# Reordering an attention layer: an earlier transpose, smaller products between row maxima, and a new prologue

## The reference, cut to what matters

```python
# layer 0, for each of B = 16 batches; x is [B, N = 1024, C = 256], adj is [N, N]; hd = C / 4 = 64
fea = transpose(x)                       # [C, N]
c_adj = mean(fea, over C)                # one number a node
A_s = a symmetric function of |c_adj[n] - c_adj[m]|     # written with sigmoid, the kernel uses tanh
g = relu((fea @ (adj * A_s)) * para)     # [C, N]
q = the four heads of transpose(g);  k, v = heads of x @ kv_w
attn = softmax(q @ k^T * scale);  out = attn @ v
x = layernorm(x + out)
# layer 1: A_hat = adj with its diagonal raised by one, normalised by degrees; agg = A_hat @ x
h = relu(batchnorm(agg @ W1^T + b1)); x = layernorm(x + batchnorm(h @ W2^T + b2))
```

## Time and profile before

| | |
|---|---|
| median of 3 runs | 3024.26 us (3023.43 to 3026.23) |
| the profiled execution | 3025.48 us, its span 3023.7 us |
| PE busy | 2794.8 us, 92% |
| PEld, DVE, ACT, POOL busy | 62%, 68%, 55%, 37% |
| mean granted TensorE clock | 0.97 of full |
| batch 3, from its first graph product to that of batch 4 | 130.03 us |

### The profile page before, as it was taken

The page is one execution under the profiler, slowest core; times in us unless marked ns, Lnnn a source line. Parts: engine busy times, 40 slices in busy tenths (PEclk is TensorE's granted clock), DMA queues, the critical chain, the costliest instruction groups (busy, mean ns, idle before and its releaser), DMA issues. The chain is left out here.

```text
span 3023.7 us, 38970 instructions
## 1 busy us (share of the span) xinstructions
PE 2794.8 (92%) x12308; PEld 1878.4 (62%) x12308; DVE 2047.3 (68%) x2981; ACT 1667.0 (55%) x2148; POOL 1127.6 (37%) x492
## 2 busy tenths in 40 slices
PE   6999999999999999999999999999499999989964
PEld 4565665656566565655656566565388888868853
DVE  5777777777777777777778777775534233338877
ACT  5666565665656666565666656564422222237768
POOL 1736446373644637355373644627200000000012
PEclk9999999999999999999999999999799999999975
DMA  4131212213122231312223121220322322305548
GB/s 132 57 105 60 83 63 73 89 57 115 56 80 69 64 111 48 102 63 73 72 74 104 59 83 63 73 76 23 112 84 98 111 83 97 111 18 185 186 161 284
DMA packets 154317, 276.19 MB, mean 91 GB/s; under 512 B 12192, under 2 KB 95136, under 8 KB 152224
## 3 DMA queue, kind: packets, MB, share of 16 engines
q1 hardware_dynamic: 154272, 275.62, 28.9%
HBM read 178.79 MB, written 62.98 MB: 80 GB/s over the span
## 5 line engine op out<-in xcount | busy, mean ns | idle before, releaser
L281 POOL TENSOR_TENSOR psum<-psum,probs 128x1024 f32<-128x1024 f32 x320 | 855.5, 2674 | 171.0 <-ACT probs L342 144.1
L342 ACT ACTIVATE probs<-sc_ps 128x1024 f32<-128x1024 f32 x512 | 507.5, 1024 | 458.6 <-PE sc_ps L779 449.7
L507 DVE TENSOR_REDUCE mx<-mx_ps 128x1 f32<-128x512 f32 x768 | 494.3, 685 | 215.3 <-PE mx_ps L747 206.1
L795 PE MATMUL pv_ps<-probs,v 128*64 128x512 f32 x2048 | 490.7, 602 | 0.0
L779 PE MATMUL sc_ps<-qa,ka 128*128 128x512 f32 x1024 | 385.7, 408 | 0.0
L779 PE MATMUL sc_ps<-qb,kb 128*128 128x512 f32 x1024 | 373.3, 395 | 6.5 <-DMA qb<-row 6.5
L281 POOL TENSOR_TENSOR psum<-probs 128x1024 f32<-128x1024 f32 x64 | 183.2, 2863 | 511.6 <-ACT probs L342 511.6
L747 PE MATMUL mx_ps<-ka,qa 128*128 128x512 f32 x768 | 288.9, 435 | 15.4 <-DVE mx L507 10.7
L795 PEld LDWEIGHTS pv_ps<-probs,v 128*64 128x64 f32 x2048 | 130.2, 137 | 232.7 <-issue 195.6
L469 DVE SCALAR_TENSOR_TENSOR scr<-scr,adj_ring 128x1024 f32<-128x1024 f32 x128 | 195.2, 1525 | 98.5 <-ACT scr L308 93.9
L747 PEld LDWEIGHTS mx_ps<-ka,qa 128*128 128x128 f32 x768 | 132.9, 187 | 203.7 <-DVE mx L507 122.8
(11 more groups left out here) (170 smaller groups left out, 5341.8 us busy)
## 6 DMA issues: line engine op xcount, KB each, us to landing
adj_ring<-in_adj_dram SPq DMA_DIRECT2D x128, 512.0 KB, 3.7
pre_scratch<-pre SPq DMA_DIRECT2D x28, 1024.0 KB, 4.9
pre<-pre_scratch SPq DMA_DIRECT2D x28, 1024.0 KB, 4.9
x<-in_x_dram SPq DMA_DIRECT2D x16, 1024.0 KB, 5.6
kb<-ka SPq DMA_DIRECT2D x64, 256.0 KB, 3.0
qa<-qa SPq DMA_DIRECT2D x64, 256.0 KB, 3.0
res<-in_x_dram SPq DMA_DIRECT2D x16, 1024.0 KB, 5.6
x_scratch<-res SPq DMA_DIRECT2D x16, 1024.0 KB, 4.5
```

The costliest lines, as they stand in the source:

```text
L281: pool.tensor_tensor(psum[:, h % 2, :], probs[:, 0, :] if k == 1 else psum[:, h % 2, :], probs[:, k % PR, :], ALU.add).then_inc(s["pool_ad ...
L342: nc.scalar.activation(probs[:, i % PR, :], sc_ps[:, t % 2, :], ACT.Exp, scale=SCALE)\
L507: nc.vector.tensor_reduce(mx2[:, nh, n:n + 1], mx_ps[:, nh, :], AX.X, ALU.max)\
L795: ins = nc.tensor.matmul(pv_ps[nh * HD:(nh + 1) * HD, h % 2, :], v[:, i, h * HD:(h + 1) * HD], probs[:, i % PR, nh * BANK:(nh + 1) * BANK] ...
```

## The change

Six edits. In head 3's preparation `xt_low(b + 1, 1)` goes ahead of `weigh(b + 1, 2)` on VectorE and `w_high(b + 1, 0)` two exponentials earlier on ScalarE. Between head 0's maxima TensorE gets single tiles of v and pieces of three matmuls of k (`k_piece`) where it had two tiles and pieces of six; one more tile of v is made behind the maxima's transpose and no tile between maxima 5 and 6. VectorE's `k_low` 2 and 3 go from ahead of head 1's maxima to behind the first and the second. `q_low(b, 1)` goes behind five of them, `q_low(b, h + 1)` from ahead of the next head's maxima to behind two. In heads 1 and 2 the second maximum goes from pair 1 to pair 0, and the first between the two parts of pair 0's scores. The prologue's instructions are reordered, and the `para` load goes behind that of the sums.

```diff
--- before.py
+++ after.py
@@ -63,7 +63,7 @@
     WR, DR, AR, PR = 3, 3, 2, 4
     PAIRS = T // 2
     MAX_FIRST = [0, 1, 1, 1]
-    MAX_MID = [0, 1, 1, 0]
+    MAX_MID = [[0, 1, 1, 0], [1, 0, 1, 0], [1, 0, 1, 0]]
     MAX_LAST = [1, 1, 1, 0]
     SUM_PAIR, DEN_PAIR, BACK_PAIR = 1, 2, 3
     POOL_ADDS = T - 2
@@ -229,8 +229,8 @@
             sp.dma_start(scr[:, 0, :].rearrange("p (c n) -> p c n", c=CT), kvw_v).then_inc(s["kvw_in"], 16)
             load_adj(0, 0)
             load_adj(0, 1)
+            spread_sums(0)
             sp.dma_start(neg_para[:, :, :], para_v).then_inc(s["para_in"], 16)
-            spread_sums(0)
             load_adj(0, 2)
             load_adj(0, 3)
             sp.wait_ge(s["kq_set"], 2 * HEADS)
@@ -380,8 +380,8 @@
                     tanh_half(b, p - 1)
                 if (h, p) == (3, 0):
                     xt_high(b, 0)
+                    w_high(b, 0)
                 if (h, p) == (3, 1):
-                    w_high(b, 0)
                     xt_high(b, 1)
                     w_high(b, 1)
                 if (h, p) == (3, 2):
@@ -431,10 +431,23 @@
                         if h and p == SUM_PAIR:
                             den_copy(b, h - 1)
 
+            x_high(0, range(T))
+            xt_high(0, 0)
+            xt_high(0, 1)
             act.wait_ge(s["consts_set"], 3)
-            for h in range(HEADS):
-                for p in range(PAIRS):
-                    prepare(0, h, p)
+            distance(0, 0)
+            tanh_half(0, 0)
+            distance(0, 1)
+            tanh_half(0, 1)
+            w_high(0, 0)
+            distance(0, 2)
+            tanh_half(0, 2)
+            w_high(0, 1)
+            k_high(0, 0)
+            k_high(0, 1)
+            w_high(0, 2)
+            distance(0, 3)
+            tanh_half(0, 3)
             over_batches(act, B, body)
             head_copy(B - 1, HEADS - 1)
             den_copy(B - 1, HEADS - 1)
@@ -580,19 +593,21 @@
                 maxima(b, 0, range(T))
                 maxima_row(b, 0)
                 q_low(b, 0)
+                maxima(b, 1, range(0, 1))
                 k_low(b, 2)
+                maxima(b, 1, range(1, 2))
                 k_low(b, 3)
-
-                maxima(b, 1, range(0, 4))
+                maxima(b, 1, range(2, 5))
                 q_low(b, 1)
-                maxima(b, 1, range(4, T))
+                maxima(b, 1, range(5, T))
                 maxima_row(b, 1)
 
                 for h in (1, 2):
-                    q_low(b, h + 1)
                     maxima(b, h + 1, range(0, 1))
                     add_last(b, h - 1)
-                    maxima(b, h + 1, range(1, 4))
+                    maxima(b, h + 1, range(1, 2))
+                    q_low(b, h + 1)
+                    maxima(b, h + 1, range(2, 4))
                     if h == 1 and not last:
                         split_x(b + 1)
                     maxima(b, h + 1, range(4, 7))
@@ -608,8 +623,8 @@
                     weigh(b + 1, 1)
                     xt_low(b + 1, 0)
                     w_low(b + 1, 0)
+                    xt_low(b + 1, 1)
                     weigh(b + 1, 2)
-                    xt_low(b + 1, 1)
                     w_low(b + 1, 1)
                 invert_sums(b, 2)
                 if not last:
@@ -619,13 +634,14 @@
                     k_low(b + 1, 1)
                 add_head(b, 2)
 
+            xt_low(0, 0)
+            xt_low(0, 1)
             split_x(0)
-            for n in range(3):
-                weigh(0, n)
-            xt_low(0, 0)
+            weigh(0, 0)
             w_low(0, 0)
-            xt_low(0, 1)
+            weigh(0, 1)
             w_low(0, 1)
+            weigh(0, 2)
             w_low(0, 2)
             weigh(0, 3)
             k_low(0, 0)
@@ -666,20 +682,27 @@
                                                   x32[:, 4 * half + q, c * P:(c + 1) * P], ident[:, :])
                 ins.then_inc(s["xt_ready"], 1)
 
-            def k_product(b, c, halves=range(NH)):
-                if c == 0:
-                    wait(pe, s["xtl_done"], 2 * b + 2)
-                    wait(pe, s["row_done"], 4 * b)
-                else:
+            def k_terms(c, nh):
+                ws = slice(c * P, (c + 1) * P)
+                cols = slice(nh * BANK, (nh + 1) * BANK)
+                return split_terms([((kvw_hi[:, k, ws], kvw_lo[:, k, ws]), (xT_hi[:, k, cols], xT_lo[:, k, cols]))
+                                    for k in range(CT)])
+
+            def k_product(b):
+                wait(pe, s["xtl_done"], 2 * b + 2)
+                wait(pe, s["row_done"], 4 * b)
+                for nh in range(NH):
+                    ins = product(mx_ps[:, nh, :], k_terms(0, nh))
+                ins.then_inc(s["k_ready"], 1)
+
+            def k_piece(b, nh, piece):
+                if nh == 0 and piece == 0:
                     wait(pe, s["res_added"], 4 * b)
-                out = (mx_ps, pv_ps)[c]
-                ws = slice(c * P, (c + 1) * P)
-                for nh in halves:
-                    cols = slice(nh * BANK, (nh + 1) * BANK)
-                    ins = product(out[:, nh, :], split_terms(
-                        [((kvw_hi[:, k, ws], kvw_lo[:, k, ws]), (xT_hi[:, k, cols], xT_lo[:, k, cols]))
-                         for k in range(CT)]))
-                if nh == NH - 1:
+                terms = k_terms(1, nh)
+                for k in range(3 * piece, 3 * piece + 3):
+                    lhsT, rhs = terms[k]
+                    ins = nc.tensor.matmul(pv_ps[:, nh, :], lhsT, rhs, start=k == 0, stop=k == len(terms) - 1)
+                if nh == NH - 1 and piece == 1:
                     ins.then_inc(s["k_ready"], 1)
 
             def v_product(b, j, tiles=range(4)):
@@ -829,27 +852,25 @@
                 if (h, p) == (3, 1):
                     transpose_x(b, 1)
                 if (h, p) == (3, 2):
-                    k_product(b, 0)
+                    k_product(b)
 
             def body(b, last):
                 g_product(b)
                 v_product(b, 0, [0, 1])
                 max_scores(b, 0, 0)
                 max_scores(b, 0, 1)
-                v_product(b, 0, [2, 3])
+                v_product(b, 0, [2])
                 max_scores(b, 0, 2)
-                k_product(b, 1, [0])
+                v_product(b, 0, [3])
                 max_scores(b, 0, 3)
-                k_product(b, 1, [1])
-                max_scores(b, 0, 4)
-                max_scores(b, 0, 5)
+                for nh in range(NH):
+                    for piece in range(2):
+                        k_piece(b, nh, piece)
+                        max_scores(b, 0, 4 + 2 * nh + piece)
                 v_product(b, 1, [0, 1])
-                max_scores(b, 0, 6)
-                max_scores(b, 0, 7)
-                v_product(b, 1, [2])
                 transpose_maxima(b, 0)
 
-                v_product(b, 1, [3])
+                v_product(b, 1, [2, 3])
                 scores(b, 0, 0, [0])
                 scores(b, 0, 1, [0])
                 for h in range(HEADS):
@@ -864,12 +885,15 @@
                         i = 2 * p
                         maxes(MAX_FIRST[p])
                         if p == 0:
-                            for part in (0, 1) if h else (1,):
-                                scores(b, h, i, [part])
-                                scores(b, h, i + 1, [part])
+                            if h:
+                                scores(b, h, i, [0])
+                                scores(b, h, i + 1, [0])
+                                maxes(MAX_MID[h][p] if more else 0)
+                            scores(b, h, i, [1])
+                            scores(b, h, i + 1, [1])
                         else:
                             scores(b, h, i)
-                            maxes(MAX_MID[p])
+                            maxes(MAX_MID[h][p] if more else 0)
                             scores(b, h, i + 1)
                         maxes(MAX_LAST[p])
                         if h and p == DEN_PAIR:
@@ -892,10 +916,10 @@
                 values(b, HEADS - 1, T - 1)
 
             pe.wait_ge(s["ident_set"], 3)
+            transpose_x(0, 0)
+            transpose_x(0, 1)
             pe.wait_ge(s["consts_set"], 3)
-            for h in range(HEADS):
-                for p in range(PAIRS):
-                    prepare(0, h, p)
+            k_product(0)
             pe.wait_ge(s["kq_set"], 2 * HEADS)
             over_batches(pe, B, body)
             sum_up(B - 1, HEADS - 1)
```

## The result

The changed kernel takes 3101.41 us (four runs, 3099.59 to 3101.71) against 3023.85 for the kernel before beside it: +77.6 us, a ratio of 1.0254, 95% interval 1.0242 to 1.0266. Forecast were 3093 us and slower. The profiled execution took 3101.47 us, its span 3099.7; TensorE is busy 2848.5 us (92%) at a mean granted clock of 0.959.

The account below looks back on a forecast made before the run. The prediction took TensorE's work plus its stops as the bound. Its terms, -34.5 + 41 + 27 + 10 + 24 - 7 + 9 = +69.5, took the profiled 3025.5 to 3095, or 3093 us as median; range 3060 to 3130.

Parts of the forecast that it names:

- C: Heads 1 and 2, two maxima a pair: `q_low` sometimes waits for GpSimd's addition, 0.75 us a head; +24 us.
- B2: Head 1's first maximum to values: `k_low` between the reductions delays the maxima, +1.7 us in 16 batches; +27 us.
- K: TensorE's clock: old falls go, -9 us; new falls ahead of head 1 cost +18; sum +9 us.
- A: Head 3's preparation: the stop ahead of the k product goes, 2.3 us in each of 15; -34.5 us.
- B1: Head 0's maxima: k 2.65 us later delays ScalarE's dense row and head 1's first maximum; +41 us.
- B3: Head 1, fifth to eighth maximum: `q_low(b, 1)` delays the reduction of maximum 5, +0.6 us; +10 us.
- The rival: Heads 1 and 2: GpSimd always first, `q_low` waits +2.6 us, `split_x` +2.4; 3149 us, chance 0.09.
- P: Prologue: earlier copies and sums bring the first v product near 53 instead of 60.07; -7 us.
- nothing late: Rival: nothing behind head 0's maxima is late, TensorE's own work decides; 2957 us, chance 0.13.
- only B1: Rival: only B1 is paid, `k_low` and `q_low` find gaps; 3015 us, chance 0.08.

Follow-up runs that it names:

- after_row: Changed kernel with head 0's row store ahead of the two copies of qa on SP; 3096.73 us, 1.0246.
- after_both: Changed kernel with head 0's row store ahead of the copies of qa and the normalising moved between head 0's exponentials; 3158.6 us, 1.0452.
- te_fill: Kernel before with TensorE's new order between head 0's maxima, plus twelve redundant matmuls in the stop before the scores' second parts; 3064.85 us, 1.0141.
- te_only: Kernel before with only TensorE's new order between head 0's maxima (single v tiles, k in pieces of three); 3107.17 us, 1.0271.
- ve_only: Kernel before with only VectorE's new places for `k_low` 2 and 3 and `q_low(b, 1)`; 3066.09 us, 1.0139.
- a_only: Kernel before with only head 3's preparation reordered (`xt_low` 1 ahead of `weigh` 2, `w_high` 0 earlier); 2980.5 us, 0.9855.
- after_norm: Changed kernel with the normalising moved from ahead of `v_copy(b, 1)` to between head 0's exponentials; 3212.65 us, 1.0632.
- c_maxima_only: Kernel before with only TensorE's two maxima a pair in heads 1 and 2, `q_low` kept in place; 3044.59 us, 1.0068.
- c_short: Kernel before with the changed maxima and `q_low` order of heads 1 and 2, GpSimd's additions cut to 64 of 1024 columns; 2971.05 us, 0.9824.

## Why the forecast held, and where it didn't

Direction and total were right (+77.6 measured, +69.5 forecast), the terms only in part. That the total came out within 8 us is partly luck: C was 14 us too small, B2 and K's new falls together 9 us too large, and these errors met. The sums below are over all batches, from the same distances as the table.

- **A, -34.5:** right in place and size, -2.46 x 15 = -37. Alone it brings -45, since the falls of the earlier trace rows go with the stop; that part of K, forecast -9, is -8.1 in the changed kernel.
- **B1, +41:** right, +40. k is complete at 11.48 instead of 8.82 behind v (+2.66, forecast 2.65), the first maximum is +2.62, `v_copy` ends 0.15 ahead of it. `after_row` leaves it where it is; `after_both` takes it away, to 1.14 below before, which is the 1.1 forecast for TensorE's own order. That the row's DMA only splits the stop held: it landed 19.2 behind v, forecast 18.7. In batch 0 I had +1.25 and it was +2.66: the row came 1.8 later, and the clock was at 1.2 GHz for the scores behind it (`te_fill`, at the full clock: +1.76).
- **B2, +27, and K's +18 of new falls:** wrong as two terms of a sum. Between first maximum and values the changed kernel loses 2.30 a batch, 36 us, and not 45. The slow clock alone makes 2.40 (`te_only`), VectorE's order alone 1.94 (`ve_only`, 32 us), and the two together no more than the larger. What the slow clock adds to `k_low` is at most 0.4 a batch (7.72 against 7.34 in `after_both`), 5 us in all, where I had 18. That isn't because the change has shorter falls: batch 8 of `te_only` and batch 3 of the changed kernel both have 6.8 us at 1.2 GHz that begin 0.4 us behind the first maximum, and it costs 2.1 us there and 0.2 here. Both delays slow the same chain, maximum, reduction, maximum, so the longer hides the shorter. Alone the new falls are worth 40 us (`te_fill`), twice my 18: I had priced a fall by the earlier trace rows, where the costlier of two slow stretches lies at the k product; here it lies on a chain of short waits.
- **B3, +10:** +0.84 x 16 = 13, and again the slow clock adds nothing to it (`te_only` has 13.54 without it).
- **C, +24:** right cause, undersized: 0.96 + 1.42 a batch, 38 us. I took the middle between "`q_low` gets in first" and "it waits" (1.3 a head), and it waits in every batch, 2.7 us long in head 1 and 2.6 in head 2. The rival had 2.6 for `q_low` and 2.4 for `split_x`; `split_x` hardly waits (2.38, less than the 2.62 of before), so that is too much.
- **P, -7:** -8.0 at batch 0's first v product; 52.05, forecast 53.
- **Sum of the parts run alone:** -44.9 + 81.8 + 40.7 + 39.1 - 7.6 = +109, against 77.6. By the distances, the parts have 41 us too many between the first maximum and head 1, which is the overlap just named, and 12 us too few behind the k product, because `a_only`, `te_only` and `ve_only` each lose clock falls there that can go only once.

Of the rivals, "nothing late" fell with the first maximum at 21.0; "only B1" described `te_fill` (+42) but not the change. Open: the last batch ends 1.3 us later behind head 3 than the stages explain. In `after_norm` and `after_both` these 1.3 us are gone (0.1), so they go when the normalising is moved, but which wait carries them wasn't followed. Open too is why `c_maxima_only` has more falls at the k product at an unchanged order there.

## What to carry to other kernels

A stop can hide a later one: before taking away the wait that the profile names, look for the next (here 3.00 us for a DMA were worth nothing while a copy on ScalarE ended later still). Moving work off an in-order engine moves everything that waits for it, so follow the DMA queue too: moving the normalising cost 112 us on top of the change and, with three DMA issues put ahead (two rows and `copy_kb`), was part of a kernel 72 us faster than before. Where two delays slow the same chain of reduction and matmul, don't add them.

## What the runs showed of the hardware

- A short stop can cost more than its length. 3.0 us of waiting in each batch brought 3.4 to 10.2 us at 1.2 GHz, and in most batches of `te_only` that added 3.7 us up to head 1. Filling the stop with 12 matmuls won 40 us. The stop of 2.21 us of the earlier trace rows was followed by a fall in 5 of 15 batches.
- A GpSimd addition and a VectorE instruction with two inputs in SBUF (`q_low`, `split_x`, the weighing) take turns. `q_low` at 505.54 took 2.71 us instead of 1.20 while the addition ran to 507.17, that is 1.63 of waiting and 1.08 of work; another addition stretched to 4.25 while `split_x` ran, to 2.26 behind its end (GpSimd, then `split_x`, changed kernel). With the additions cut short in `c_short`, `q_low` takes 1.21 and the weighing 1.22:

```profile
504.79 2.38 POOL L281 TENSOR_TENSOR psum<-probs 128x1024 f32<-128x1024 f32 x1 [3.48 <-ACT probs L342]
...
511.04 4.25 POOL L281 TENSOR_TENSOR psum<-psum,probs 128x1024 f32<-128x1024 f32 x1 [0.16 <-POOL psum L281]
```

```profile
510.65 2.38 DVE L468 TENSOR_TENSOR x_lo<-x,x_hi 128x2048 fp32r<-128x2048 f32 x1
```
